# Graph kernel: first edge pass by ranges of 32 nodes, and each group of edges gathered once

## The chip, the cores and the metric

The kernel runs on one core of a Trainium2 chip. Its metric is the device time of one execution in microseconds (us). The engines are PE (TensorE, matrix products; PEld is its weight load), DVE (VectorE), ACT (ScalarE), POOL (GpSimd) and SP (SyncE, which here only issues DMAs). Each engine runs its own list of instructions in order; semaphores tie them together. SBUF is the memory on the chip with 128 partitions, PSUM the eight banks that PE writes.

## What is computed

A graph with 3125 nodes of 128 features and 100,000 edges, sorted by destination in the input, with 64 features an edge. Two message-passing layers, each followed by a residual and a layer norm:

```python
h = x @ node_fc_W + node_fc_b;  he = ea @ edge_fc_W + edge_fc_b
hs, hd = h[src], h[dst]
a = sum(hs * hd, -1)                                    # one score an edge
g = sigmoid(relu(he @ rel_att_W1[m] + b1[m]) @ W2[m] + b2[m])   # m = 0..2
alpha, beta = seg_softmax(a, dst), seg_softmax(g, dst)
h_att = segment_sum(alpha * (hs @ node_att_W[k]), dst) / 3      # over k
h_rel = segment_sum(beta[m] * (hs @ rel_att_W[m]), dst) / 3     # over m
h_red = relu(concat(h_att, h_rel) @ out_fc_W + out_fc_b)
gate = sigmoid(x @ gate_W + gate_b)
x1 = layernorm(x + gate * where(deg > 0, h_red, h) + (1 - gate) * x)
# second layer: edges are summed by src, rows are gathered by dst
e = tanh((x1 @ Wq)[src] + (x1 @ Wk)[dst]);  s = exp(e @ Wphi - max)
out = layernorm(x1 + segment_sum(s / z[src] * ((x1 @ Wy_w + Wy_b)[dst] + e @ We), src))
```

## The kernel before

**Stages, one after the other.** Stage 1 (from L182): SP loads weights, edges and x; 25 blocks of 125 nodes go through `h = x @ W` (PE L470 to L486) and are stored as rows (`h_table`, L372) and transposed (`hT_table`, L373); then the edge MLP runs over 100 octs of 1000 edges (PE L526, L536, L547, ACT L667), which gives three weights an edge. Beside it DVE sorts the edges' keys by source for the second pass (with PE transposes, L564), and counts how many edges belong to nodes below each block's border (L769, 25 passes over the edges), from which a plan of steps is made. The edges' records of 10 words (source, destination, weights as floats and as three bf16 parts) are written to DRAM as `rec0` by five stores (L378), each behind conversions (L853 to L857).

**First edge pass** (L923 to L1155). Edges are in groups of 512 (4 x 128); a step is one group against one block of 125 nodes. Since the edges are sorted, a group crosses few borders: 196 groups and 25 blocks give 196 + 25 - 1 = 220 steps, and a group that crosses a border is loaded and gathered again for the next block. In a step
- SP loads the group's records `rec` and the block's transposed `h`, `hbT` (L972, L973);
- POOL gathers the 512 source rows of `h_table` into `hs` with four indirect DMAs of 128 rows (L984; `hs` has RING = 5 slots in the `arena`), and waits before it until step n - 5 is done (`stepped`);
- DVE makes the one-hot matrix edge to node, `onehot` (L1101, L1104), the one-hot weighed by three relation weights, 128 x 1500 (`weigh`, L1111), the running maximum (`maximum`, L1121 to L1130), and adds the step's sums to the block's (`take`, L1140 to L1145);
- PE transposes the rows (L1000) and the one-hot (L1006), computes scores of 125 nodes x 512 edges (L1017), transposes the exponentials (`turn_back`, L1022), and sums: relations 4 x 375 columns (L1030), their weights' sums (L1033), attention 4 x 129 columns (L1039);
- ACT copies the transposed rows to SBUF (`hsT`, L1061), makes the mask (L1063), copies the transposed exponentials (L1069), and takes the exponentials (L1073, L1075).

The order on PE in one iteration k is `turn_back(k)`, `turn(k+2)`, `scores(k+1)`, `relations(k)`, `attention(k)`. Every step is one iteration of a loop that is written out 10 times.

**Between the passes** (L1160 to L1403): the node update, the layer norm, and the tables of the second layer: `kv_table` with 192 floats a node, and `q_table`.

**Second edge pass** (L1408 to L1676). Again 220 steps, now with the edges sorted by source. SP loads `rec_sb` and `qb` (L1468, L1469); POOL gathers 4 x 128 rows of `kv_table` (L1482) into `row_v` (5 slots), again with waits for the step's records and for step n - 5. PE transposes the one-hot (L1498, copied by ACT L1572), spreads the queries (L1511), DVE adds them to the gathered rows (L1617), ACT takes the tanh (L1552), DVE the scores and the highest of them (L1633 to L1639, L1625) with a transpose and a broadcast on PE (L1518, L1522), ACT the exponentials (L1562 to L1567), DVE spreads them (`spread_p`, L1646), PE sums the messages (L1528), DVE adds them up (`take`, L1658). The tail (L1681 to L1809) normalises and stores the output (L1718).

## Time and profile before

| what | value |
|---|---|
| median of the runs | 3890.93 us (3888.9 to 3900.16, 3 runs) |
| the profiled execution | 3869.89 us, of it 3868.0 us span in the trace |
| mean granted TensorE clock | 0.837 of full speed |

The profile is of one execution. It has a page with busy times per engine, a digit strip over the span, the costliest groups of instructions, and the DMA queues; the trace behind it can be asked for the instructions of a stretch (a timeline), for busy times by stretch (windows), for what each engine waited for (waits). Busy shares of an engine are averages over stages that have different limits. "issue" as releaser means that the engine waited for nothing that the profile shows; "remote" that a semaphore released it whose setter the profile can't name.

### The profile page before, as it was taken

Reading aid. Unit: us, or ns where it says so; the run is one execution under the profiler, and the core shown is the slowest. Engines: PE = TensorE matmul, PEld = TensorE weight load, DVE = VectorE, ACT = ScalarE, POOL = GpSimd, SP = SyncE. Lnnn points to the kernel's source line nnn. Section 1 sums busy time; section 2 is a strip of 40 time slices with the busy share of each in tenths; the row PEclk is TensorE's granted clock in tenths of the full one; section 3 lists DMA queues with packets and bytes.
Section 4 is the critical chain, followed back from the end, with each engine's and each line's share of the span. In section 5 each row is a group of like instructions: output and inputs, shape, how many; then the busy total and the mean of one; then the engine's idle time right before and its main releaser. Section 6 shows DMA issues by size and latency. Waiting matters only on the chain. (4 is left out here: it accounts for less than half of the span.)

```text
span 3868.0 us, 66746 instructions
## 1 busy us (share of the span) xinstructions
PE 2980.1 (77%) x17025; PEld 2039.3 (53%) x17025; DVE 2193.4 (57%) x5947; ACT 1479.6 (38%) x3759; POOL 1902.0 (49%) x1791
## 2 busy tenths in 40 slices
PE   5999999698989889898889936665665666656663
PEld 3444333466666666666666634554554555545552
DVE  8455210566666656666656673655555555555554
ACT  3777776233333334333333322222222222222221
POOL 0000000566666656666656502666666666666660
PEclk9999999799999989999999965776667777677675
DMA  2111121212212112222212102222222222222220
GB/s 69 57 45 45 55 76 39 60 48 52 52 49 50 50 47 52 49 52 51 49 48 50 39 2 60 72 70 70 70 71 72 70 70 71 71 71 72 71 69 19
DMA packets 231858, 217.93 MB, mean 56 GB/s; under 512 B 161623, under 2 KB 190124, under 8 KB 231787
## 3 DMA queue, kind: packets, MB, share of 16 engines
q0 software_dynamic: 70400, 144.29, 14.0%
q1 hardware_dynamic: 161387, 72.74, 7.5%
q8 instruction: 38, 0.62, 0.1%
q14 instruction: 33, 0.27, 0.0%
HBM read 203.65 MB, written 13.22 MB: 56 GB/s over the span
## 5 line engine op out<-in xcount | busy, mean ns | idle before, releaser
L984 POOL DMA_INDIRECT arena<-h_table,rec x880 | 976.4, 1110 | 545.8 <-issue 249.9
L1482 POOL DMA_INDIRECT arena<-kv_table,rec_sb x880 | 911.8, 1036 | 471.7 <-issue 235.3
L1030 PE MATMUL bank<-arena 128*128 128x375 f32 x1760 | 611.3, 490 | 0.0
L1528 PE MATMUL bank<-arena,probT 128*125 128x193 f32 x1760 | 513.8, 456 | 122.3 <-DVE probT L1646 65.6
L1528 PEld LDWEIGHTS bank<-arena,probT 128*125 128x125 f32 x1760 | 422.8, 265 | 179.7 <-DVE probT L1646 103.3
L1030 PEld LDWEIGHTS bank<-arena 128*128 128x128 f32 x1760 | 349.4, 199 | 302.0 <-issue 122.6
L1522 PE MATMUL bank<-top_run,ones 1*128 1x1 f32 x440 | 108.6, 313 | 367.8 <-DVE top_run L1625 196.4
L1111 DVE TENSOR_TENSOR arena<-onehot,rec 128x1500 f32<-128x1500 bf16 x220 | 376.5, 1711 | 0.0
L536 PE MATMUL bank<-eaT,wc 64*128 64x500 f32 x1200 | 360.8, 616 | 0.0
L1572 ACT COPY hotT<-bank 125x512 bf16<-125x512 bf16 x220 | 128.1, 582 | 580.4 <-remote 514.3
L1126 DVE CUSTOM_DVE_ANT_0 score<-bank,mask,m_old 125x512 f32<-125x512 f32 x220 | 165.2, 751 | 296.3 <-remote 178.8
L1522 PEld LDWEIGHTS bank<-top_run,ones 1*128 1x128 f32 x440 | 89.9, 253 | 453.2 <-DVE top_run L1625 243.1
L667 ACT ACTIVATE arena<-bank,bias 128x500 f32<-128x500 f32 x534 | 314.6, 684 | 36.6 <-PE bank L536 32.3
L977 POOL MEMSET arena<- 128x20 f32 x1 | 0.1, 134 | 649.5 <-POOLq L328 649.5
L1069 ACT COPY probT<-bank 128x500 f32<-128x500 f32 x220 | 126.8, 576 | 439.3 <-PE bank L1022 309.4
L1073 ACT ACTIVATE prob<-score,m_neg 125x512 f32<-125x512 f32 x220 | 158.8, 722 | 343.4 <-DVE m_neg L1129 308.6
L1022 PE MATMUL bank<-identf,prob 125*128 125x125 f32 x880 | 146.5, 292 | 165.5 <-issue 95.2
L1017 PE MATMUL bank<-hsT,hbT 128*125 128x512 f32 x440 | 272.0, 704 | 0.0
L1039 PE MATMUL bank<-arena,probT 128*125 128x129 f32 x1760 | 248.6, 283 | 0.0
L1617 DVE TENSOR_TENSOR arena<-bank,arena 128x256 f32<-128x256 f32 x220 | 92.7, 421 | 245.3 <-remote 235.9
L536 PEld LDWEIGHTS bank<-eaT,wc 64*128 64x128 f32 x1200 | 133.1, 186 | 164.1 <-ACT arena L667 105.9
L1646 DVE TENSOR_TENSOR probT<-onehot,p_e 128x500 f32<-128x500 bf16 x220 | 149.7, 680 | 115.9 <-ACT p_e L1565 80.1
(291 smaller groups left out, 4881.7 us busy)
## 6 DMA issues: line engine op xcount, KB each, us to landing
ea<-in_edge_attr SPq DMA_DIRECT2D x100, 250.0 KB
arena<-h_table,rec POOLq DMA_INDIRECT x880
arena<-kv_table,rec_sb POOLq DMA_INDIRECT x880
hbT<-hT_table SPq DMA_DIRECT2D x220, 62.5 KB
qb<-q_table SPq DMA_DIRECT2D x220, 46.9 KB
rec<-rec SPq DMA_DIRECT2D x220, 20.0 KB
rec<-rel_st SPq DMA_DIRECT2D x5, 781.2 KB
rec_sb<-rec SPq DMA_DIRECT2D x220, 4.0 KB
```

The costliest lines, as they stand in the source:

```text
L536: pe.matmul(bank[1 + (6 * o + n) % 4][:, 0:4 * LANES], wc[half * DE:(half + 1) * DE, m * D:(m + 1) * D], eaT[half * DE:(half + 1) * DE, o ...
L667: act.activation(hid[o % 3 * 6 + n], bank[1 + (6 * o + n) % 4][:, 0:4 * LANES], ACT.Relu, bias=bias1[:, m:m + 1]).then_inc(hid_sb, 1)
L984: pool.indirect_dma_start(out=hs[:, k % RING, j, 0:D], out_offset=None, in_=h_table, in_offset=bass.IndirectOffsetOnAxis(ap=rec_v[:, k, j, ...
L1017: pe.matmul(bank[2][0:BN, :], hbT[:, k, :], hsT[:, k % 2, :], start=True, stop=True).then_inc(score_ps, 1)
L1030: pe.matmul(bank[6 + k % 2][:, 0:M * BN], hs[:, k % RING, j, 0:D], hot_w_v[:, k % 2, j, :], start=(j == 0), stop=(j == GT - 1))
L1039: last = pe.matmul(bank[4 + k % 2][0:BN, 0:D + 1], probT_v[:, k % 2, j, :], hs[:, k % RING, j, :], start=(j == 0), stop=(j == GT - 1))
L1073: act.activation(prob[:, k % 2, :], score[:, k % 2, :], ACT.Exp, bias=m_neg[:, k % 2:k % 2 + 1]).then_inc(prob_done, 1)
L1111: v.tensor_tensor(hot_w[:, k % 2, :].rearrange("p (j m n) -> p j m n", j=GT, m=M), onehot_v[:, k % RING, :, :].unsqueeze(2).to_broadcast([ ...
L1126: v.tensor_tensor_reduce(score[:, q, :], bank[2][0:BN, :], mask[:, q, :], 1.0, m_old[:, q:q + 1], ALU.add, ALU.max, m_new[:, q:q + 1]).the ...
L1482: pool.indirect_dma_start(out=row_v[:, k % RING, j, 0:KV], out_offset=None, in_=kv_table, in_offset=bass.IndirectOffsetOnAxis(ap=rec_v[:, ...
L1522: pe.matmul(bank[3][:, 0:1], ones[0:1, :], top[0:1, k:k + 1], start=True, stop=True).then_inc(top_ps, 1)
L1528: last = pe.matmul(bank[4 + k % 2][0:BN, 0:KV + 1], probT_v[:, k % 2, j, :], row_v[:, k % RING, j, AD:RK], start=(j == 0), stop=(j == GT - 1))
```

## The change

**Nodes in blocks of 128.** BN is 128 in place of 125, 25 blocks, the last one part full; tables have 3200 rows. In the x phase each block has 4 ACT copies instead of 6, with PSUM banks for two blocks.

**Edge records stay in SBUF.** Sources, destinations and weights of all edges lie in SBUF by group (`src_g`, `dst_g`, `w_g`); the record stores and conversions are gone. SP loads `dst_g` and `src_g` in runs of 4 words, 128 x 195 runs for each, right behind the first four loads of edge features and ahead of the stores of `h_table` and `hT_table`; ACT waits for all of those stores before the edge MLP. The MLP runs over 98 octs of 1024 edge slots. The counting passes are 98 (one a range border) instead of 25.

```diff
-                        sp.dma_start(ea[:, k, :], ea_dram[:, o * 8 * DE:(o + 1) * 8 * DE]).then_inc(ea_in[k], 16)
+                        def load_group(table, name):
+                            sp.dma_start(table[:, 0:COLS - GT].rearrange("p (g j) -> p g j", j=GT),
+                                         i[name][0:FULL].rearrange("(g p j) -> p g j", p=128, j=GT)).then_inc(groups_in, 16)
...
+                        for o in range(U):
+                            load_edges(o)
+                        load_group(dst_g, "dst")
+                        load_group(src_g, "src")
+                        for b in range(NB):
+                            sp.wait_ge(hT_sb, b + 1)
+                            sp.dma_start(h_table[b * BN:(b + 1) * BN, :], h_sb[:, b, :]).then_inc(h_out, 16)
+                            sp.dma_start(hT_table[:, b * BN:(b + 1) * BN], hT[:, b, :]).then_inc(h_out, 16)
```

**First pass by ranges of 32 nodes.** A step is one group against one of 98 ranges of 32 nodes: 196 + 98 - 1 = 293 steps, rounded up to 296 (`STEPS0`). POOL goes over the 196 groups, written out, and gathers each once into a ring of 16 landed groups (`RING0`, `landed_rows`); before group g it loads from `reach_row` the last step that uses group g - 16 and waits for it. SP copies a step's rows by DMA from the ring into one of 8 step slots (`hs`, 128 x 516 floats) and loads 32 columns of `hT_table`:

```diff
+                        groups = sp.value_load(plan_s[0:1, bass.ds(n, 1), 0], min_val=1, max_val=GROUPS)
...
+                        sp.wait_ge(stepped, n + SU0 - SH + 1)
+                        sp.wait_ge(ready, groups)
...
+                        sp.dma_start(hbT[:, k, :], hT_table[:, bass.ds(within(col, (WINS - 1) * WN), WN)]).then_inc(step_in[k], 16)
+                        sp.dma_start(hs[:, k, :, :].rearrange("p j d -> p (j d)"),
+                                     landed_rows[:, bass.ds(within(at, (RING0 - 1) * GT), GT), :].rearrange("p j d -> p (j d)")).then_inc(step_in[k], 16)
```

On PE the scores' tile is 32 x 512. The mask is made in PSUM by two products ahead of the scores (a constant from `far`, and the one-hot times a large diagonal), so ACT's mask is gone. The probabilities (32 columns a group of 128) and the one-hot weighed by three relation weights (96 columns) stand side by side in `both`, and one product a quarter gives all sums of the step, 128 x 129:

```diff
+                        pe.matmul(tile, far[0:1, 0:WN], far[0:1, WN:], start=True, stop=False)
+                        for j in range(GT):
+                            pe.matmul(tile[:, j * 128:(j + 1) * 128], onehot_v[:, k % SH, j, :], big_ident[:, :], start=False, stop=False)
+                        pe.matmul(tile, hbT[:, k % SH, :], hsT[:, k % 2, :], start=False, stop=True).then_inc(score_ps, 1)
...
+                            last = pe.matmul(bank[4 + k % 4][:, 0:D + 1], both[:, k % 4, j, :], hs[:, k % SH, j, :],
+                                             start=(j == 0), stop=(j == GT - 1))
```

The order on PE in iteration k is `turn_back(k+1)`, `scores(k+3)`, `turn(k+4)`, `sums(k)`. ACT takes the exponentials straight from PSUM. DVE makes a 128 x 128 one-hot and a 128 x 384 weighed one, takes the minimum of the negated scores (one instruction), and has one sum to add instead of three. What stands in a row on PE, before:

```order
L1030 MATMUL bank<-arena 128x375 x4
L1033 MATMUL bank<-rec,onehot 125x9 x4
L1039 MATMUL bank<-arena,probT 125x129 x4
L1022 MATMUL bank<-identf,prob 128x125 x4
L1000 MATMUL bank<-identf,arena 128x128 x4
L1004 REGISTER_ALU
L1006 MATMUL bank<-identb,onehot 125x128 x4
L1017 MATMUL bank<-hsT,hbT 125x512
```

and now (`big_ident` is the diagonal, `hs` the step's rows):

```order
L1026 MATMUL bank<-identf,prob 128x32 x4
L1034 REGISTER_ALU
L1037 MATMUL bank<-far 32x512
L1039 MATMUL bank<-big_ident,onehot 32x128 x4
L1040 MATMUL bank<-hsT,hbT 32x512
L1048 MATMUL bank<-identf,hs 128x128 x4
L1056 MATMUL bank<-hs,both 128x129 x4
```

The relations' 375 columns and their sums have left the iteration, and the constant's product has come in. On POOL in the first pass, before, the gathers of two steps:

```order
L984 DMA arena<-h_table,rec 128x128 x4
L981 REGISTER_ALU
L984 DMA arena<-h_table,rec 128x128 x4
L981 REGISTER_ALU
L984 DMA arena<-h_table,rec 128x128 x4
```

and now the gathers of two groups:

```order
L1007 TENSOR_LOAD reach_row
L1007 ISA x2
L1008 REGISTER_ALU
L997 DMA area_b<-h_table,src_g 128x128 x4
L1007 TENSOR_LOAD reach_row
L1007 ISA x2
L1008 REGISTER_ALU
L997 DMA area_b<-h_table,src_g 128x128 x4
```

Each set of four gathers has a value load ahead of it; a step no longer has a set of its own.

**Second pass.** The 220 steps stay. POOL gathers each of the 196 groups once into a ring of 8 (`RING1`), with the sources of indices loaded once (`rec_all`), and SP moves a step's rows by DMA (128 x 4 x 192 floats) into the `row_v` slots; DVE's `add_queries` waits for that DMA (`moved`).

```diff
-                            pool.wait_ge(loaded[k], 32 * s + LOADS0 + 32)
-                            pool.wait_ge(stepped, s * SU + k + SU - RING + 1)
...
+                        sp.wait_ge(stepped, n + SU - RING + 1)
+                        sp.wait_ge(ready, groups)
...
+                        sp.dma_start(row_v[:, k % RING, :, 0:KV], landed_rows[:, bass.ds(at, GT), :]).then_inc(moved[k % RING], 16)
...
-                        v.wait_ge(gathered[k % RING], 64 * turn_of(s, k) + GATHERS0)
+                        v.wait_ge(moved[k % RING], 16 * turn_of(s, k))
```

On SP, one step before (the loads of records and queries with the values they need):

```order
L1465 TENSOR_LOAD plan_row1
L1465 ISA x2
L1466 ISA
L1466 TENSOR_LOAD plan_row1
L1466 ISA x2
L1467 REGISTER_ALU
L1468 ISA
L1468 DMA rec_sb<-rec 128x8
L1469 ISA
L1469 DMA qb<-q_table 125x192
```

and now the part that stands behind the same loads of the step five ahead:

```order
L1433 DMA qb<-q_table 128x192
L1437 ISA
L1437 TENSOR_LOAD plan_l
L1437 ISA x2
L1438 ISA
L1438 TENSOR_LOAD plan_l
L1438 ISA x2
L1442 ISA
L1442 DMA sum_acc<-sum_acc 128x4x192
```

The move of the rows (named `sum_acc` after the area that holds both rings) is a third DMA on SP's queue in each step, with two more value loads.

**Between and after.** The node update transposes four sums a block (the relations are in rows of the same area), accumulates four products in PSUM and adds the bias once, in place of a chain of four additions a block. The output is stored as 24 blocks of 128 nodes and one of 53.

## Rows read from the trace of the kernel before

**Rows 1.** Page, busy time, share of the span, instructions.
```profile
PE 2980.1 (77%) x17025; PEld 2039.3 (53%) x17025; DVE 2193.4 (57%) x5947; ACT 1479.6 (38%) x3759; POOL 1902.0 (49%) x1791
```

**Rows 2.** Windows: stretch, length, busy of PE, PEld, DVE, ACT, POOL, PEclk, DMA share, GB/s.
```profile
100.00:655.00 555.00, 550.20 (x2880) 221.56 (x2880) 183.60 (x329) 406.35 (x727) 0.00 (x0) 1.00 0.17 54
697.00:2224.00 1527.00, 1358.02 (x7476) 974.11 (x7476) 975.80 (x2419) 578.47 (x1100) 970.21 (x874) 0.93 0.20 50
2390.00:3787.00 1397.00, 879.68 (x5939) 721.08 (x5940) 804.47 (x2638) 396.89 (x1540) 911.68 (x880) 0.71 0.27 70
```

**Rows 3.** Timeline of PE in the first pass: start, duration, engine, line, what, [idle before].
```profile
1604.53 1.09 PE L1022 MATMUL bank<-identf,prob 125*128 125x125 f32 x4 [4.12 <-issue]
...
1611.65 0.59 PE L1022 MATMUL bank<-identf,prob 125*128 125x125 f32 x4
1612.07 0.60 PE L1000 MATMUL bank<-identf,arena 128*128 128x128 f32 x4
1612.51 0.39 PE L1006 MATMUL bank<-identb,onehot 128*125 128x128 bf16 x4
1612.74 1.07 PE L1017 MATMUL bank<-hsT,hbT 128*125 128x512 f32 x2
1613.65 2.69 PE L1030 MATMUL bank<-arena 128*128 128x375 f32 x8
1616.18 0.34 PE L1033 MATMUL bank<-rec,onehot 128*125 128x9 bf16 x4
1616.38 1.13 PE L1039 MATMUL bank<-arena,probT 128*125 128x129 f32 x8
1617.35 0.59 PE L1022 MATMUL bank<-identf,prob 125*128 125x125 f32 x4
```

**Rows 4.** Waits: engine, what, its line, releaser: us in total, times, longest.
```profile
ACT hotT L1572 <- remote: 514.3, 107, 8.4
...
POOL arena L1482 <- remote: 182.8, 86, 3.7
...
PE bank L1022 <- issue: 95.2, 33, 4.4
```

**Rows 5.** Page, groups of gathers: busy us, mean ns of one, idle before.
```profile
L984 POOL DMA_INDIRECT arena<-h_table,rec x880 | 976.4, 1110 | 545.8 <-issue 249.9
L1482 POOL DMA_INDIRECT arena<-kv_table,rec_sb x880 | 911.8, 1036 | 471.7 <-issue 235.3
```

**Rows 6.** Timeline of POOL in the first pass.
```profile
1408.64 1.65 POOL L984 DMA_INDIRECT arena<-h_table,rec  x1 [0.30 <-issue]
```

**Rows 7.** Timeline of all engines in the second pass.
```profile
2997.73 0.42 PE L1498 MATMUL bank<-identb,onehot 128*125 128x128 bf16 x4
...
3002.23 0.95 POOL L1482 DMA_INDIRECT arena<-kv_table,rec_sb  x1 [0.30 <-issue]
...
3006.01 0.59 ACT L1572 COPY hotT<-bank 125x512 bf16<-125x512 bf16 x1 [5.86 <-remote]
...
3006.92 1.27 POOL L1482 DMA_INDIRECT arena<-kv_table,rec_sb  x1 [2.49 <-remote]
```

**Rows 8.** Timeline of PE at the end of the second pass, behind POOL's last gather.
```profile
3779.39 1.57 PE L1528 MATMUL bank<-arena,probT 128*125 128x193 f32 x8 [0.65 <-DVE probT L1646]
...
3782.70 1.57 PE L1528 MATMUL bank<-arena,probT 128*125 128x193 f32 x8 [0.23 <-DVE probT L1646]
```

**Rows 9.** Page, the group of the weighed one-hot on DVE.
```profile
L1111 DVE TENSOR_TENSOR arena<-onehot,rec 128x1500 f32<-128x1500 bf16 x220 | 376.5, 1711 | 0.0
```

**Rows 10.** Timeline of SP: a load that blocks its queue, and the output store.
```profile
13.15 15.59 SPq L353 DMA_DIRECT2D w<-in_L_gnn_rel_att_W  x1
...
3851.40 0.31 SPq L1718 DMA_DIRECT2D out<-y_sb  x1
```

**Rows 11.** Page, DMA queue of SP: packets, MB, share of 16 engines.
```profile
q1 hardware_dynamic: 161387, 72.74, 7.5%
```

**Rows 12.** Timeline of DVE at the end of stage 1.
```profile
683.85 0.06 DVE L1091 MEMSET neg_big<- 125x1 f32 x1 [8.53 <-PEq L328]
```

1316 lines of the change are left out of this document (651 added, 665 removed).

## Prediction

> **What bounds the kernel now.** I read the page's busy shares first: TensorE is busy 77% of the span [rows 1]. An average over unlike stages says little, so the second look was at the busy times by stage [rows 2]. In the edge MLP (100 to 655 us) PE is busy 550 of 555 us: PE binds. In the first edge pass (697 to 2224) PE is busy 1358 of 1527 us at a mean granted clock of 0.93, POOL 970; in the second pass (2390 to 3787) PE has 880 of 1397 us at 0.71 and POOL 912: neither is full. So each pass needs the timeline of its steps.
>
> A first-pass step that waits for nothing shows each matmul group by its start [rows 3]: 0.42 for the probability transposes (L1022), 0.44 for the row transposes (L1000), 0.23 and 0.91 for one-hot transposes and scores, 2.53 for the three relations (L1030), 0.20 for their sums and 0.97 for the attention, together 5.70 us. 220 such steps would make 1254 us; the stage took 1527, that is 6.9 a step. The missing 1.2 us a step are slower steps and pauses like that ahead of 1604.53, where PE sat for 4.12 us and the profile names no releaser [rows 3]; there are 33 of this kind at that line, 95 us in all [rows 4].
>
> What are they? POOL issues a gather of 128 rows in 1.110 us on average in the first pass and 1.036 in the second [rows 5], and 0.30 us lies between two [rows 6]: at least 4 x 1.34 = 5.4 us of a step is POOL's own. The second pass shows best how the others fare in that time [rows 7]: the one-hot transposes at 2997.73 take 0.42 us, yet ACT, free for 5.86 us, copies their result only at 3006.01, 7.9 us after they ended. POOL issued its gathers back to back the whole time and resumes at 3006.92, after 2.49 us of rest. The waits repeat it: the copy L1572 waits 107 times for a "remote" release, 514 us in total, and POOL waits 86 times, 183 us [rows 4]. Once POOL has issued its last gather, the same steps follow each other in 3.3 us (from 3779.39 to 3782.70) [rows 8]. I read this as a release by PE that arrives late while POOL issues without a rest. The second pass is then bound by POOL's 5.3 us plus a share of late releases (6.3 us a step), the first by PE's 5.7 us plus some.
>
> **First pass, the change.** Steps go from 220 to 296 (196 groups and 98 ranges of 32 nodes, less one, rounded up to a multiple of 8); 3 of them are empty. PE per step, by the rows of [rows 3]: four probability transposes have 32 output columns instead of 125 (at least a quarter of 0.42, at most all: I take 0.25); the K=1 matmul that adds the far constant has 512 columns in bf16 (the 0.23 of four 128-column bf16 groups: 0.21), the one-hot product is of the same size as the one-hot transposes (0.22); scores 0.91, since the 512 columns stay; row transposes 0.44; the sums are 4 x 129 columns as the attention is, 0.97, and now hold relations and attention stacked in the 128 rows: the 2.53 + 0.20 go. Sum 3.0 us, x 296 = 888 us against 1254, at full clock. Behind a pause, at the lower of the two clocks, L1022 takes 1.09 us in place of 0.59 [rows 3]; at a mean clock of 0.71, as in the second pass now, PE would need about 4.1 us a step.
>
> POOL: 196 groups in place of 220 steps, so 784 gathers: 784 x (1.110 + 0.30) = 1105 us. Each group adds a value load and its waits; the trace has none on POOL, and I take 0.5 us, between one gap of 0.30 us and two (bounds 0.3 and 0.7): 1203 us (1164 to 1242). DVE had 976 us for 220 steps [rows 2], 4.4 each, of which 1.71 is the weighing of 1500 elements a lane [rows 9]; it now has 384, and there is one sum instead of three: under 3 us, not a bound. The rows' copy from the landing ring (264 KB a step, 78 MB in all) is on SP's queue; the DMA engines are busy 0.20 of the stage [rows 2] and the copy would at most double or treble that. SP issues two DMAs and three loads a step, some 2 us by 0.31 us for an issue [rows 10] and as much for a load with its register work: hidden, and a bound only above 4 us.
>
> Ends of the range per step: POOL alone 1203/296 = 4.06; the late releases on top. In a step the path PE turn, ACT copy, PE scores, DVE minimum, ACT exp, PE transposes, ACT copy, PE sums is spread over four iterations, so each release may be late by about one iteration less the work without a stall. POOL now waits for nothing before 16 groups, so it has fewer rests than today, which speaks against the change. I take 4.3 us a step, near POOL's floor, because PE's pauses are few today (33 at L1022 in 220 steps) in spite of POOL: 1273 us. From 1527 that is **-254** (bounds -345 by POOL without slowing by DVE, to +515, the rival D).
>
> One rule bears on POOL's term. The row at 1408.64 shows a gather of 1.65 us between gathers of 0.95 us [rows 6]. The Trainium skill ("SBUF — State Buffer", section "SBUF: two separate sides") says that VectorE operations in a two-port mode keep GpSimd from writing the descriptors of its DMAs. No row here shows which operation did it, but the 1.71-us weighing would be the candidate, and it becomes a quarter as long: by the rule POOL's gathers shrink to 784 x 1.25 = 980 us, by the row's mean they stay at 1105. The sum uses 1105.
>
> **Second pass.** PE, ACT and DVE do the same per step; POOL's 880 gathers become 784, 784 x (1.036 + 0.30) = 1047 us, + 196 x 0.5 = 1145. The gathers no longer wait for a step's records nor for the step five before it, but for the group eight before it; between gather and use stands a DMA of 393 KB a step (86 MB), issued by SP behind the loads of the step five ahead. With 3.3-us steps possible without POOL [rows 8], POOL's stream is the floor: 1145/220 = 5.2 us. Late releases hold up the steps, and now POOL does not rest with them until the ring of eight is full, so part of the 183 us of rests [rows 4] goes and part comes back as waits of PE. I take 5.6 us a step with the ramp, 1252 in place of 1397: **-145** (bounds -226 at POOL's floor, 0 if the loop's late releases set the pace as now).
>
> **Ahead of the first pass.** Group loads of dst and src now stand on SP's queue ahead of the 50 stores of h, and ACT waits for all those before the edge phase. They are 2 x 24,960 runs of 16 bytes. SP's queue moved 161,387 packets in 7.5% of 16 engines' span [rows 11]: 28.8 ns a packet, which gives 49,920 x 28.8 / 16 = 90 us; packets that small should cost less than the mean, so 45 to 90, and I take 67. They are issued at about 32 us (the queue is blocked to 28.7 by one load [rows 10]) and land at 99; 50 stores at 0.31 to 0.5 us behind them end near 124. The edge phase starts at 100 today: +25 (-15, if the shorter x phase sets it, to +50). The Trainium skill ("DMA: Bandwidth & Descriptors", sections "Specifications" and "Measured") wants runs of 512 bytes for line rate and gives a floor of about 10.5 ns a packet; 33 us by that as an estimate, and the edge phase would begin 10 us early. No row shows 16-byte runs. The MLP has 98 x 1024 edge slots for 100 x 1000: +2. The last conversions and store of the records (DVE idles 8.53 us for it [rows 12]) go: -10. Counting is now 98 passes over the edges instead of 25; DVE is idle for 371 of the 555 us of the MLP [rows 2] and hides them. Sum **+17** (-25 to +45).
>
> **Between the passes and after.** The 166 us between the windows [rows 2] lose the relation matmuls of the node update and gain transposes: **-15** (-30 to +5). The output store, from 3851.40 to the end at 3868 [rows 10], has 128 partitions for 125, and its 16.6 us should come nearer to half: **-8** (0 to -10).
>
> **Sum.** 17 - 254 - 15 - 145 - 8 = -405 against the span 3868: 3463. The profiled execution (3869.89) is 21 us below the median of the runs: forecast **3480**. Measurements of this kernel can tell 0.3% (12 us) from no change.
>
> **Rivals.**
> B, POOL's stream is all there is: both passes at its floor with fewer slow gathers, first pass 1182 and second 1171. 3868 + 17 - 345 - 15 - 226 - 8 = 3291, about **3300** with the offset. For it: the pauses of PE are few in today's first pass [rows 4]; against: the late releases [rows 7].
> C, the second pass gains nothing: its steps wait for PE's releases, and those come when POOL rests, however few groups it gathers. 3868 + 17 - 254 - 15 - 8 = 3608, **3630**.
> D, the slower side: a late release costs its time per step, not per group. If a first-pass step stays at 6.9 us as today, because POOL issues on and the scores wait for ACT's copy that waits for PE's release, 296 of them are 2042 us, +515; 3868 + 17 + 515 - 15 - 145 - 8 = 4232, **4250**. It decides from where the pass grows over 1527 + 151 us, that is from 5.7 us a step. For it: [rows 7], 7.9 us for one release; against: PE's own 5.70-us rhythm [rows 3] breaks seldom today with two iterations of lead [rows 4], and the new order has four.
> E, gains and costs about cancel (steps of 5.6 to 5.7 us).
>
> **Chances.** Forecast 0.44 (its own range 3380 to 3570), B 0.19, C 0.22, D 0.11, E 0.04 (0.03 of it within 0.3%, the rest faster). Faster by over 0.3% 0.86, within 0.03, slower 0.11. The range 3280 to 3700 leaves out D, E and a little of B.
>
> **What would show it.** The first pass over 296 steps at 4.1 to 4.6 us with POOL busy nearly without gaps, PE groups without L1030's 2.5 us, PE clock under 0.9: right. Steps above 5 us with ACT's copy of the turned rows (the old L1061) waiting for "remote": D's mechanism. A second pass of 1397 us or more: C. The first edge matmul later than 150 us or earlier than 85: the group loads are mis-sized. The row copies binding would show as a DMA share over 0.8, and SP's issue rows without a pause. Most wrong would be the take of 4.3 us, which rests on how long a release is late, and no row prices that for four iterations of lead.

## The result, and the profile after

The changed kernel takes 4143.58 us (median of 4 runs, 4118.61 to 4162.02) where the kernel before takes 3889.91 us (median of 4): a ratio of 1.0644, with a 95% interval of 1.0569 to 1.0719. It is slower by 6%; 3480 us had been forecast, and the time lies outside the range of 3280 to 3700.

In the experiments the same two kernels also ran on other chips, and there the change is a gain. **c_after** took 3112.51 us (median) beside 3387.46 us for the kernel before (ratio 0.919, interval 0.9174 to 0.9205). The experiments ran on four chips: on two of them the kernel before took 3388 to 3396 us, on the other two, and on the chip of the result, 3843 to 3890. I call the second kind "chips with late releases", for the reason that follows; the prediction rests on a trace of that kind, and so does the result above. Of the experiments, those without an interval were run once.

So there are four traces to read: before and after on a chip of each kind. One group of matmuls a step marks the passes: the attention sums (L1039), now the joint sums (L1056), and the messages (L1528, now L1525). Each row gives the shortest, median and longest duration in ns, then the start of the first and the last. The kernel before, late releases:
```profile
L1039 PE MATMUL bank<-arena,probT x1760: 271/273/354, 712.8 to 2223.3; 128*125 128x129 f32 x196
L1528 PE MATMUL bank<-arena,probT x1760: 324/528/688, 2413.2 to 3787.1; 128*125 128x193 f32 x196
```
The changed kernel, late releases:
```profile
L1056 PE MATMUL bank<-hs,both x2368: 272/275/423, 766.5 to 2428.0; 128*128 128x129 f32 x198
L1525 PE MATMUL bank<-sum_acc,probT x1760: 324/528/691, 2638.1 to 4086.9; 128*128 128x193 f32 x196
```
The changed kernel on a chip without late releases (c_after):
```profile
L1056 PE MATMUL bank<-hs,both x2368: 272/275/422, 706.0 to 1692.1; 128*128 128x129 f32 x198
L1525 PE MATMUL bank<-sum_acc,probT x1760: 324/528/691, 1870.3 to 3037.5; 128*128 128x193 f32 x196
```
The kernel before on the same chip (c_before):
```profile
L1039 PE MATMUL bank<-arena,probT x1760: 271/273/354, 713.0 to 1960.7; 128*125 128x129 f32 x196
L1528 PE MATMUL bank<-arena,probT x1760: 324/528/687, 2143.3 to 3303.8; 128*125 128x193 f32 x196
```
By their medians the single matmuls are equally long on both kinds, only the spans differ. In us, a pass from the first to the last start, divided by 219 steps (220 less one) or, in the new first pass, by 295:

| | late: before | late: after | without: before | without: after |
|---|---|---|---|---|
| first sums at | 713 | 767 | 713 | 706 |
| first pass | 1510 (6.90 a step) | 1662 (5.63) | 1248 (5.70) | 986 (3.34) |
| from there to the first messages | 190 | 210 | 183 | 178 |
| second pass | 1374 (6.27) | 1449 (6.62) | 1161 (5.30) | 1167 (5.33) |
| from there to the end | 81 | 73 | 81 | 73 |
| span | 3868 | 4160 | 3385 | 3111 |

The columns add up: with late releases the change costs 54 + 151 + 20 + 75 - 8 = +292 us, without them it gives -7 - 262 - 4 + 7 - 8 = -274.

Busy times by stage, the changed kernel with late releases, then without (columns as in [rows 2]):
```profile
698.00:2428.00 1730.00, 1240.53 (x6801) 752.35 (x6799) 538.16 (x1475) 519.02 (x1479) 760.23 (x763) 0.76 0.24 77
2584.00:4087.00 1503.00, 969.88 (x5940) 784.91 (x5940) 810.05 (x2638) 404.30 (x1541) 782.98 (x784) 0.65 0.40 117
```
```profile
698.00:1692.00 994.00, 988.61 (x6792) 625.66 (x6793) 539.65 (x1472) 494.44 (x1479) 736.12 (x764) 1.00 0.44 133
1846.00:3037.00 1191.00, 857.24 (x5936) 683.04 (x5937) 802.84 (x2639) 417.04 (x1541) 803.01 (x786) 0.75 0.52 147
```
Without late releases PE is busy 988.61 of 994 us in the first pass, at full clock. With them it has 1240.53 of 1730 us at 0.76: the same matmuls, with pauses and, behind the pauses, a lower clock. The waits of the changed kernel with late releases (columns as in [rows 4]):
```profile
ACT hotT L1569 <- remote: 555.4, 141, 6.6
...
DVE junk L1133 <- remote: 527.2, 82, 29.3
...
ACT hsT L1079 <- remote: 485.5, 78, 29.4
...
DVE sum_acc L1614 <- DMA sum_acc<-sum_acc: 450.5, 188, 35.4
```
In the first pass DVE waits 527.2 us for scores and ACT 485.5 us for turned rows, and in the second ACT waits another 555.4 us, each time for a release that the profile can put down to no setter. In c_after and c_before no wait has "remote" as its releaser at all.

The start of the first pass shows most plainly what a late release is. POOL has 16 free slots there and issues 64 gathers one behind the other, every 1.25 us, from 671.7 to 752. The changed kernel with late releases, SP and DVE in that time (timeline of SP, then of all engines):
```profile
708.21 0.69 SPq L983 DMA_DIRECT2D hbT<-hT_table  x1
...
726.57 0.70 SPq L983 DMA_DIRECT2D hbT<-hT_table  x1
...
731.67 0.74 DVE L1133 TENSOR_SCALAR_CACHE_REDUCE junk<-bank,m_old 32x512 bf16<-32x512 f32 x1 [29.26 <-remote]
...
742.85 0.59 ACT L1079 COPY hsT<-bank 128x512 f32<-128x512 f32 x1 [29.44 <-remote]
...
768.49 1.25 POOL L997 DMA_INDIRECT area_b<-h_table,src_g  x1 [16.50 <-PE bank L1056]
```
SP, which waits for nothing here, needs 18.36 us from one step's `hbT` load to the next (708.21 to 726.57); DVE waits 29.26 us for scores whose matmul started at 713.48, and ACT, free since 713.42, copies only at 742.85 what PE turned from 729.41 to 730.50. At 768.49 POOL has waited 16.50 us for a step. The same place without late releases:
```profile
697.10 0.35 SPq L983 DMA_DIRECT2D hbT<-hT_table  x1
...
700.08 0.35 SPq L983 DMA_DIRECT2D hbT<-hT_table  x1
```
2.98 us from load to load, with POOL gathering all the same. The record of the trace also holds SP's register instructions, which the timeline leaves out: between the two loads at 708.21 and 726.57 nearly all of them last 0.69 to 0.73 us each, where the same ones, but for the value loads, last 0.02 to 0.16 us between 697.10 and 700.08 in c_after. What of a chip makes the difference I don't know. The gathers themselves are alike, 995 ns on average with late releases (page, busy us and mean ns) and 964 in c_after:
```profile
L997 POOL DMA_INDIRECT area_b<-h_table,src_g x784 | 780.3, 995 | 1538.1 <-issue 871.3
```

### The profile page after: what moved, and what is told of

It is laid out like the page before. It is cut to its first block and busy times, and to the rows that moved or that the text cites. A ratio compares the mean times of both kernels' runs of the same rounds, so it can differ in the third digit from the quotient of the medians.

```text
span 4160.4 us, 66648 instructions
## 1 busy us (share of the span) xinstructions
PE 2957.8 (71%) x16380; PEld 1891.6 (45%) x16380; DVE 1804.8 (43%) x5054; ACT 1411.6 (34%) x4020; POOL 1575.7 (38%) x1602
## 5 line engine op out<-in xcount | busy, mean ns | idle before, releaser
L997 POOL DMA_INDIRECT area_b<-h_table,src_g x784 | 780.3, 995 | 1538.1 <-issue 871.3
L1465 POOL DMA_INDIRECT sum_acc<-kv_table,rec_all x784 | 783.6, 1000 | 686.1 <-PE bank L1525 405.4
L1525 PE MATMUL bank<-sum_acc,probT 128*128 128x193 f32 x1760 | 597.0, 514 | 30.6 <-DVE probT L1643 19.4
L1133 DVE TENSOR_SCALAR_CACHE_REDUCE junk<-bank,m_old 32x512 bf16<-32x512 f32 x296 | 218.4, 738 | 815.6 <-remote 527.2
L1525 PEld LDWEIGHTS bank<-sum_acc,probT 128*128 128x128 f32 x1760 | 498.8, 309 | 95.2 <-DVE probT L1643 73.1
L1040 PE MATMUL bank<-hsT,hbT 128*32 128x512 f32 x592 | 399.6, 765 | 0.0
L1056 PE MATMUL bank<-hs,both 128*128 128x129 f32 x2368 | 365.8, 304 | 0.0
L678 ACT ACTIVATE sum_acc<-bank,bias 128x512 f32<-128x512 f32 x588 | 351.3, 696 | 40.3 <-PE bank L557 35.9
L557 PE MATMUL bank<-area_b,wc 64*128 64x512 f32 x1176 | 362.8, 635 | 0.2 <-ACT sum_acc L678 0.2
L1056 PEld LDWEIGHTS bank<-hs,both 128*128 128x128 f32 x2368 | 346.9, 224 | 0.9 <-issue 0.8
L1569 ACT COPY hotT<-bank 128x512 bf16<-128x512 bf16 x220 | 128.9, 586 | 608.9 <-remote 555.4
L1048 PE MATMUL bank<-identf,hs 128*128 128x128 f32 x1184 | 244.7, 342 | 53.0 <-DMA hs<-area_b 26.6
```

The lines of the kernel that those rows point to most:

```text
L557: pe.matmul(bank[1 + (6 * o + n) % 4][:, :], wc[half * DE:(half + 1) * DE, m * D:(m + 1) * D], eaT[half * DE:(half + 1) * DE, o % 3, :], s ...
L678: act.activation(hid[o % 3 * 6 + n], bank[1 + (6 * o + n) % 4][:, :], ACT.Relu, bias=bias1[:, m:m + 1]).then_inc(hid_sb, 1)
L997: pool.indirect_dma_start(out=landed_rows[:, k * GT + j, 0:D], out_offset=None, in_=h_table, in_offset=bass.IndirectOffsetOnAxis(ap=src_g[ ...
L1040: pe.matmul(tile, hbT[:, k % SH, :], hsT[:, k % 2, :], start=False, stop=True).then_inc(score_ps, 1)
L1048: last = pe.transpose(bank[0][:, j * 128:(j + 1) * 128], hs[:, k % SH, j, 0:D], identf[:, :])
L1056: last = pe.matmul(bank[4 + k % 4][:, 0:D + 1], both[:, k % 4, j, :], hs[:, k % SH, j, :], start=(j == 0), stop=(j == GT - 1))
```

## The experiments

Theory A: while POOL issues gathers one behind the other, releases and instructions of the other engines are held up on some chips. Theory B: a step's own chain is the bound. For the second pass, theory S: SP's list of instructions fills the step; theory M: the latency of the row move. The two passes are separated by a barrier, so one kernel can carry an edit in each. Runs with the same time of the kernel before beside them ran on one chip; each section names its kind by that time. e1, e2, f1 and g3 leave out work (most gathers), so their sums are of old rows: only their times are read.

**e1, no gathers** (3388 us beside it, no late releases). Edit, in the first pass, and with `RING1` in the second:

```diff
+                        if g >= RING0:
+                            return
```

> The changed kernel, but POOL issues gathers only for the first 16 groups of the first pass and the first 8 of the second; later groups keep their waits and their release, so the rows used are stale (work left out: 720 and 752 gathers). Theory A (POOL's back-to-back gathers hold up the releases and the instructions of every other engine, SP's above all): behind the first 16 groups a first-pass step takes 3.1 us, as now in intervals without a gather, so from the first scores to the last sums some 70 + 290 x 3.1 = 970 us instead of 1730; a second-pass step takes 3.3 to 4 us, 730 to 880 us instead of 1449; total near 2750. Theory B (the step's own chain, its row copy by DMA and SP's instructions, is the bound, and the gathers only run beside it): the first pass stays above 1500 us, the second above 1300, total above 3900.

3094 us. First and second pass:
```profile
L1059 PE MATMUL bank<-hs,both x2368: 272/275/377, 705.8 to 1685.7; 128*128 128x129 f32 x198
L1531 PE MATMUL bank<-sum_acc,probT x1760: 324/528/690, 1865.7 to 3019.4; 128*128 128x193 f32 x196
```
3.32 and 5.27 us a step, but c_after has 3.34 and 5.33 with all gathers. On this chip they cost nothing, so A wasn't tested; what the run shows is B for this kind of chip, and that the second pass has a bound of 5.3 us that is not POOL. Here it shows on SP's queue, with one row move in each step:
```profile
2501.61 0.67 SPq L1445 DMA_DIRECT2D sum_acc<-sum_acc  x1
...
2506.84 0.67 SPq L1445 DMA_DIRECT2D sum_acc<-sum_acc  x1
```
5.23 us from row move to row move, the pace of the pass.

**e2, memsets for gathers** (same chip). As e1, with nine (seven) memsets of the slot in place of a group's gathers.

> As e1, but in place of the left-out gathers POOL fills the group's slot with memsets, nine a group in the first pass and seven in the second, about the 5 us that four gathers take. Theory A with the descriptor writing of the gathers as cause: steps as short as in e1 unless POOL's own pace (about 5 us a group, 980 us a pass) binds, so 1000 to 1100 us a pass. Theory A with POOL's mere being busy, or its turning of the ring, as cause: near the changed kernel, 1730 and 1449 us.

3367 us; 3.96 and 5.65 us a step. POOL's memsets, chained by waits, take 6.0 us a group where four gathers take 5.07, and set the first pass. Nothing was held up on this chip, so this run says nothing of A either.

**e3, a rest behind each gather** (same chip).

```diff
+                            rested_n[0] += 1
+                            pool.memset(rest, 0.0).then_inc(rested, 1)
+                            pool.wait_ge(rested, rested_n[0])
```

> The changed kernel with a rest of POOL behind each gather: a memset of 256 words and a wait for it, some 0.35 us, so that two gathers never follow at once. Theory A: releases of the others get through in the rests; the gathers take 784 x 1.6 us = 1250 plus 100 for value loads, and the first pass becomes 1350 to 1450 us instead of 1730 although POOL does more; second pass 1350 to 1450 instead of 1449. Theory B, or a POOL that holds others up in proportion to its gathers: no shorter than now, or longer by up to 270 us a pass.

3913 us, 4.98 and 6.75 us a step: slower, since nothing was held up here and POOL binds. Four gathers take 7.5 us instead of 5.07 (784 of them from 670.5 to 2148.5); I read this as its sequencer no longer running ahead.

**e4, offset gathers, and the old gather in the second pass** (same chip).

```diff
+                            if j == 2 and last_step is not None:
+                                pool.wait_ge(stepped, last_step + SU0 + 2)
...
-                        if inside(edge, k, 0):
-                            move_rows(s, k)
...
+                            pool.wait_ge(stepped, s * SU + k + SU - RING + 1)
+                            for j in range(GT):
+                                pool.indirect_dma_start(
+                                    out=row_v[:, k % RING, j, 0:KV], out_offset=None, in_=kv_table,
```

> Two edits in stages that are separated by a barrier. First pass: the last two gathers of a group wait one step longer than the first two, so that runs of gathers are shorter. Theory A: 1350 to 1650 us instead of 1730; theory B: 1730. Second pass: the old way, four gathers a step straight into the step's slot (880 instead of 784), and no row moves on SP's queue. If the second pass lost by the row move and what SP does for it, it is back at 1371 us from its first to its last messages (1449 now); if blocks of 128 nodes or anything else costs it, it stays near 1449.

3105 us. The second pass took 1163 us with the old gathers and 1167 with ring and row moves: where POOL's gathers had taken 5.3 us (four of 1.018 us and 0.30 us behind each, c_before), SP's list now takes as long. What surprised more was the first pass, 3.34 us, far below what I had read in the trace, and the 3388 us of the kernel before. That led to the next two.

**c_after, c_before** (3387 us, no late releases). No edit.

> The changed kernel unchanged, as the measure for the four runs before it, beside which the kernel before took 3388 us where it had taken 3890. In the experiment with offset gathers no engine waited for a late release and SP's instructions took 0.04 us beside gathers, where the changed kernel's trace has 0.70. If that comes from the edit (shorter runs of gathers), this run has steps of 5.6 us in the first pass and 6.6 in the second, and takes some 4140 us, 1.2 times the kernel before beside it or more. If it comes from where or when it ran, the late releases are gone here too: 3.34 us a step in the first pass, 5.3 in the second, near 3110 us, 0.92 of the kernel before.

> The kernel before, for its trace beside that of c_after. If it takes 3388 us again and the 500 us are the late releases, then the first pass has 5.7 us a step nearly throughout (1254 us in all, not 1510) and the second about 5.3 (1165, not 1371), and waits for remote releases are near nil. If the 500 us are something else (clock, a faster stage 1), those passes are as long as in the first trace.

3112.51 and 3387.17 us: the late releases were gone in both kernels, and the edits of e4 had no part in it.

**e5 and e6, SP's list shorter and longer** (3889 us beside them: late releases).

```diff
-                            g = sp.value_load(plan1_row[0:1, bass.ds(n * 2, 1)], min_val=0, max_val=GROUPS - 1)
-                            b = sp.value_load(plan1_row[0:1, bass.ds(n * 2 + 1, 1)], min_val=0, max_val=NB - 1)
+                            g, b = values(mybir.EngineType.SP, plan1_row[0:1, bass.ds(n * 2, 2)], GROUPS - 1)
```

> The changed kernel; in the second pass SP reads group and block of the next step with one load of two values instead of two loads. In the trace of c_after SP never waits in the second pass: its list of some 30 instructions fills 5.3 us a step, and without any gather (e1) a step takes 5.26 too. Theory S (SP's list is the bound there): 0.9 us less of it gives 4.4 us, and then POOL's gathers bind at 784 x 1.27 / 220 = 4.5 us: second pass 1000 to 1050 us instead of 1167, total near 2960 to 3000 where the changed kernel takes 3112. Theory M (the latency of the row move, or the chain through the step five back, is the bound): 1167 us as now.

```diff
+                        for _ in range(2):
+                            sp.value_load(plan_s[0:1, bass.ds(n, 1), 0], min_val=1, max_val=GROUPS)
...
+                        sp.value_load(plan_l[0:1, bass.ds(n, 1), 0], min_val=1, max_val=GROUPS)
```

> The changed kernel with loads on SP whose values nobody uses: two more a step in the first pass (about 0.6 us each), one more in the second. Theory S: second pass 5.3 + 0.6 = 5.9 us a step, +130 us; first pass, where SP's list fills 2.95 of 3.34 us, goes to 4.1 to 4.2 us a step, +230 us; total near 3470, slower than the kernel before. Theory M, SP hidden: no change, 3112.

The expectations were for the other kind of chip, so the passes have to be set beside the changed kernel with late releases. e5 took 4047.97 us (ratio to before 1.0421, interval 1.0366 to 1.0476), e6 4310.71. Their messages, e5 and then e6:
```profile
L1535 PE MATMUL bank<-sum_acc,probT x1760: 324/528/691, 2601.8 to 3975.0; 128*128 128x193 f32 x196
```
```profile
L1528 PE MATMUL bank<-sum_acc,probT x1760: 324/528/690, 2672.0 to 4235.5; 128*128 128x193 f32 x196
```
Second pass 1373 and 1564 us against 1449: one load less gives 76 us, one more costs 115. That is S, on this kind of chip too. How far such passes scatter from run to run shows in the first pass, which e5 leaves as it is (1645 us, the changed kernel 1662), and in f4 below, which has e5's second pass (1351 us, e5 1373): some 20 us. In the first pass e6 took 1692 us: two loads more cost 30 to 47 us, so there SP's list is not the bound on this kind of chip. For comparison with f4, e5's first pass:
```profile
L1056 PE MATMUL bank<-hs,both x2368: 272/275/423, 765.1 to 2410.5; 128*128 128x129 f32 x198
```

**f1, no gathers, merged load** (3850 us beside it: late releases). e1's and e5's edits.

> As e1 (gathers only for the first 16 groups of the first pass and the first 8 of the second, the rest left out) with SP's merged load of e5. Chips differ: some show late releases beside gathers (the kernel before takes 3890 us there), some do not (3388 us). Where they do, theory A (the gathers' issue holds up the others' releases and instructions) says: without gathers both passes run as on the other chips, 3.32 us a step in the first, 4.4 in the second, total near 2900 us, against 4048 for the same kernel with gathers. If such a chip is slow for another reason, the passes stay above 5 us a step. On a chip without late releases: first pass 3.32 us as in e1, second 4.4 us (5.26 in e1) if SP's list is its bound, total near 2910.

2923.3 us; the kernel with gathers (e5) takes 4048.
```profile
L1059 PE MATMUL bank<-hs,both x2368: 272/275/398, 764.0 to 1744.0; 128*128 128x129 f32 x198
L1541 PE MATMUL bank<-sum_acc,probT x1760: 324/327/691, 1932.1 to 2848.4; 128*128 128x193 f32 x196
```
3.32 and 4.18 us a step: on a chip with late releases, without gathers, the first pass runs as on the other kind. Theory A holds there, B falls. In the second pass the gathers cost 457 us (1373 in e5, 916 here), far more than the 76 us of a load. The first sums still come at 764.0, since the 16 first groups were gathered in one run: 58 us later than the 705.8 of e1. The second pass at 4.18 us instead of e1's 5.27 is S again, with less on SP's list.

**f3, a short rest** (same chip). A memset of one word a partition behind each gather, without a wait.

> The changed kernel with the merged load, and behind each gather a memset of one word a partition on POOL, so that gathers follow each other at about 1.4 us instead of 1.25. Where releases are late, theory A: a short rest lets them through; the first pass is bound by POOL at 784 x 1.4 = 1100 us, 3.7 to 4.2 us a step instead of 5.6, the second 5.0 to 5.8 instead of 6.3; total 3450 to 3700 instead of 4048. Rival A2 (releases are late in proportion to the gathers, rests change nothing): 4048 or more. On a chip without late releases: slower than without the rest, 3.75 us a step in the first pass (+120 us).

4048.67 us (ratio 1.0514, interval 1.0482 to 1.0545), the time of e5 (first pass 1684 us, second 1346). The memset was no rest:
```profile
1500.36 0.95 POOL L998 DMA_INDIRECT area_b<-h_table,src_g  x1 [0.19 <-issue]
1501.31 0.11 POOL L1002 MEMSET area_b<- 128x1 f32 x1
1501.61 0.94 POOL L998 DMA_INDIRECT area_b<-h_table,src_g  x1 [0.19 <-issue]
```
It fits into the 0.30 us that lie between gathers anyway, which still start every 1.25 us. The run says nothing of rests.

**f4, offset gathers, merged load** (same chip). e4's first edit and e5's.

> The changed kernel with the merged load, and in the first pass the last two gathers of a group wait one step longer than the first two. Where releases are late, theory A: shorter runs of gathers, first pass 4.2 to 5.2 us a step instead of 5.6; total 3750 to 3950 instead of 4048. Rival A2: 4048. On a chip without late releases: first pass 3.34 us as before (e4), second pass 4.5 to 4.7 us instead of 5.3 by theory S, total near 2960 to 2990 and the fastest of all so far; by theory M 3112.

3819.6 us (ratio 0.9901, interval 0.9865 to 0.9936): first pass 1459 us, 4.94 us a step, where e5 has 1645.
```profile
L1060 PE MATMUL bank<-hs,both x2368: 272/275/423, 763.7 to 2222.3; 128*128 128x129 f32 x198
```
Behind the first sums POOL's gathers come in 191 runs of 3.8 on average (counted from the timeline, a run ending at a pause of 0.5 us or more), in e5 in 108 runs of 6.7. The same gathers in shorter runs cost 186 us less.

**g1 and g3, e3 and e2 again** (3843 us beside them: late releases).

> The same kernel as e3 (a memset of 256 words and a wait for it behind each gather, no other edit), in the hope of a chip with late releases; on the chip without, its steps took 4.97 us in the first pass and 6.74 in the second, bound by POOL. The short rest of f3 was none: the one-word memset fitted into the 0.30 us that lie between gathers anyway, which went on every 1.25 us. Where releases are late: if a real rest of some 0.6 us lets them through (A), the passes are as on the other chip, 4.97 and 6.7 us a step (the first 0.6 less than the changed kernel's 5.6). If the releases are held by the gathers in proportion (A2), it is slower than the changed kernel in both passes, above 6 us a step in the first.

3915.61 us, where e3 took 3913 on the other kind, and the passes are alike too, 1471 and 1477 us against 1468 and 1477. With a real rest behind each gather the difference between the chips is gone. Even the first sums come at 711.1 behind the same 64 gathers (710.8 in e3). POOL in g1, with a gather every 1.55 us in a group and a longer pause between groups:
```profile
1501.24 0.95 POOL L999 DMA_INDIRECT area_b<-h_table,src_g  x1 [0.27 <-POOL area_b L1003]
1502.19 0.33 POOL L1003 MEMSET area_b<- 128x256 f32 x1
1502.79 0.95 POOL L999 DMA_INDIRECT area_b<-h_table,src_g  x1 [0.27 <-POOL area_b L1003]
...
1507.14 0.95 POOL L999 DMA_INDIRECT area_b<-h_table,src_g  x1 [1.53 <-issue]
```

> The same kernel as e2 (POOL busy with memsets about as long as the gathers, which are left out behind the first groups). On the chip without late releases: 3.96 us a step in the first pass, 5.64 in the second, first sums at 708 us. Where releases are late: if it is the gathers' own work that holds releases up, the same 4.0 and 5.6 us; if any busy POOL does, 5.6 and 6.6 us as in the changed kernel.

3403.61 us against 3367 for e2; 3.83 and 5.59 us a step, with waits for a remote release only at the real gathers that open the passes. A busy POOL holds nobody up; gathers in a row do. Whether it is their issue or their transfers that does it, no run separates. The 64 gathers at the start are real in this kernel, and its first sums come at 767.0 (708.4 in e2).

**g2, gathers spread over the steps, and h2, the same again.** g2 ran beside g1 (3843 us, late releases), h2 beside 3396 us (no late releases). With the merged load of e5:

```diff
                         for j in range(GT):
+                            ahead = 4 * g + j - 40
+                            if ahead > 0:
+                                pool.wait_ge(stepped, SU0 + ahead * STEPS0 // (GT * GROUPS) + 1)
+                                pool.sem_inc(ticks, 1)
```

> The changed kernel with the merged load, and POOL's gathers spread over the steps: gather q of a pass waits until (q - 40) x 296/784 steps are done in the first pass, (q - 24) x 220/784 in the second, so at most three gathers follow each other in the first pass, and the burst of 64 at its start is gone. Where releases are late: A says 3.7 to 4.3 us a step in the first pass (5.6 in the changed kernel), 5.3 to 5.9 in the second, the start of the pass 40 us shorter; total 3450 to 3650, under the kernel before by 5 to 10%. A2 says no gain over f4 (3820). On a chip without late releases: 3.34 to 3.5 and 4.6 to 4.8 us a step, total 2970 to 3030.

> g2 again. On a chip with late releases 3680 to 3710 us, 0.96 of the kernel before, as measured. On a chip without (kernel before 3388 us): first pass 3.34 to 3.5 us a step, second 4.6 to 4.8, total 2970 to 3030, 0.88 to 0.89 of the kernel before, which would make it the fastest on both kinds of chip; if the waits for steps hold POOL up there, 3112 (the changed kernel) or more.

g2: 3695.96 us, ratio 0.9607 (0.9548 to 0.9666). h2: 2993.28 us, ratio 0.8813 (0.8797 to 0.8828).
```profile
L1060 PE MATMUL bank<-hs,both x2368: 272/275/423, 737.3 to 2143.0; 128*128 128x129 f32 x198
L1543 PE MATMUL bank<-sum_acc,probT x1760: 324/528/690, 2331.3 to 3626.4; 128*128 128x193 f32 x196
```
```profile
L1060 PE MATMUL bank<-hs,both x2368: 272/275/377, 708.3 to 1691.2; 128*128 128x129 f32 x198
L1543 PE MATMUL bank<-sum_acc,probT x1760: 324/328/690, 1866.1 to 2916.2; 128*128 128x193 f32 x196
```
With late releases the first pass takes 1406 us (1645 in e5) and the second 1295 (1373). Without them 983 and 1050: the waits for steps cost nothing, and 5.33 us a step in the second pass became 4.79, inside what S had given (4.6 to 4.8); since the gathers cost nothing on this chip, I put it down to SP's shorter list, though no run here had the shorter list without the spreading. On both kinds of chip this is the fastest version of those that do all the work. With late releases it took 46 us more than the top of the forecast: the runs of gathers are 3.4 long on average in the first pass, but runs of five to seven still occur (POOL, g2):
```profile
1499.35 1.24 POOL L1001 DMA_INDIRECT area_b<-h_table,src_g  x1 [1.89 <-PE bank L1060]
...
1504.64 0.94 POOL L1001 DMA_INDIRECT area_b<-h_table,src_g  x1 [0.30 <-issue]
1507.70 0.94 POOL L1001 DMA_INDIRECT area_b<-h_table,src_g  x1 [2.12 <-remote]
```

**h1, spread gathers with a rest** (beside h2, no late releases).

> g2 with a real rest behind each gather, a memset of one word and a wait for it: by g1's rows (0.95 gather, 0.33 memset, 0.27 idle) some 1.33 us from gather to gather instead of 1.25, and about 1.2 us more at each group's end, since POOL's sequencer can no longer run ahead: 6.5 us a group. Where releases are late: in g2 some remain (80 waits of DVE for a remote release, 331 us). A says the rests let them through, and POOL's pace binds: 6.5 x 196/296 = 4.3 us a step in the first pass (4.76 in g2), 5.8 in the second (5.91), total near 3540 to 3600 where g2 takes 3696. If the rest is too short to help: 3700 or more. On a chip without late releases: slower than g2, 4.3 and 5.8 us a step, near 3300.

4246.95 us (ratio 1.2507, interval 1.2484 to 1.253), far from the 3300 expected: the gathers now start every 1.9 us:
```profile
1504.87 0.94 POOL L1003 DMA_INDIRECT area_b<-h_table,src_g  x1 [0.83 <-POOL area_b L1007]
...
1506.76 0.94 POOL L1003 DMA_INDIRECT area_b<-h_table,src_g  x1 [0.83 <-PE bank L1065]
```
I had taken the pause behind the memset from g1's rows, 0.27 us; with two waits between two gathers it is 0.83. Whether a cheaper rest would take away what is left in g2 stays open.

## Why the prediction was wrong

**The reading of the bound was right, and its price was wrong.** I had read in the trace of before that PE's releases come late while POOL issues without a rest [rows 7]; f1, g1 and g3 show for the changed kernel that releases are late behind gathers in a row. Then I took 4.3 us a step for the first pass, 0.24 us over POOL's floor of 4.06, "because PE's pauses are few today". That is the step that failed: a step takes 5.63 us, and of these 2.29 are the price of late releases, with the lower clock behind their pauses (0.76 against 1.00), since it takes 3.34 where none is late. The pauses that I had counted were those of one engine at one line (33 at L1022, 95 us); in the same trace DVE alone waited longer for late scores:
```profile
DVE score L1126 <- remote: 178.8, 46, 9.2
```
The price was in my own text. PE's 5.70 us were 1.2 short of the measured step, and c_before, with 5.70 us a step, shows that these 1.2 us were what late releases cost the old kernel. On top of the floor they would have given 4.06 + 1.2 = 5.3 us a step and 1557 us, no gain in this pass. I had also called PE the old pass's bound alone; POOL's four gathers are as long (4 x 1.41 = 5.6 us), and in c_before POOL never pauses for 0.5 us between the first sums and the last.

**Why a step pays 2.29 us now and paid 1.2 before stays open.** I had written that POOL "has fewer rests than today, which speaks against the change". In number it does: behind the first sums its first-pass gathers come in 108 runs, 6.7 long on average and at most 8 but for the 64 that open the pass, where the kernel before has 155 runs of 5.6, the longest 20. f4 and g2 show that more and shorter runs help. But in sum POOL rests longer than before, 669 us against 316, because it waits for the steps. Before and now, both with late releases:
```profile
POOL arena L984 <- PE bank L1039: 195.6, 87, 5.2
```
```profile
POOL area_b L997 <- PE bank L1056: 642.2, 92, 16.5
```
And in the second pass the runs became shorter (from 6.7 to 4.2 on average) while the step became longer. So the length of the runs is not the whole of it. The new step also hangs on a row copy by SP, whose own instructions are held up, has another order on PE and little more than half of PE's work; no run separates these, gives the ring the old depth, or takes the gathers out of the kernel before.

**Rival D came nearest, with a chance of 0.11.** Its sign appeared: ACT's copy of the turned rows waits for "remote", 78 times. Its price did not: 78 such waits in 296 steps are not one a step, and a step does not stay at 6.9 us. From the first to the last sums it is 5.63 us; by the window that D was reckoned in (1527 us, now 1730, which takes in the later start) it is 5.8, just past D's point of decision at 5.7. The forecast gain of the second pass, which D kept, did not come either: it took 75 us more. That 4144 us lie near D's 4250 is therefore in part luck. Of the 1049 us between the spans of the two columns "after" of the table, the kernel before has 483: what late releases cost in all has more than doubled.

**First pass, term by term.** Where releases are not late, -262 us were measured and -254 forecast, which is luck: the forecast goes from 6.9 us a step to 4.3, that chip from 5.70 to 3.34. PE's step was forecast at 3.0 us and is 3.34. POOL's floor was too high: a group takes 5.07 us (784 gathers from 672.2 to 1665.7 in c_after), so the 0.5 us for a value load and waits was nothing, and I read this as POOL's sequencer doing them while a gather is being issued. (The bound of -345 in the prediction can't be got from its terms: gathers of 980 us and 98 for the groups make 1078, which is -449.) And gathers became shorter, 1121 ns in c_before and 964 in c_after (1110 and 995 with late releases). The change also shortened VectorE's weighing of the one-hot, from 1711 to 552 ns. The Trainium skill ("SBUF — State Buffer", "SBUF: two separate sides") says that GpSimd is kept from writing its DMA descriptors while VectorE runs an operation that takes the shared port pair. That would fit; no run shortened the weighing alone, so it is not shown.

**Second pass: -145 forecast, +75 with late releases, +7 without.** I costed POOL and left SP at nothing, a second term that failed. The row move put a third DMA and two value loads on its list, which fills 5.3 us a step, as much as POOL's gathers had. Where no release is late, e1 shows this bound (5.27 us with no gathers); f1, again without gathers but with one load less, has 4.18 us, and h2 agrees. Where releases are late, e5 and e6 move the pass with the list, but the gathers weigh more (457 us between e5 and f1). SP's instructions themselves are held up there: of its some 3940 register instructions in this pass 7.6% last 0.5 us or more, in c_after none, and they add up to 410 us against 245. The step grew to 6.62 us. My rival C (no gain, because the steps wait for late releases) gave the right size where none is late, for another reason; where they are late its reason is not excluded.

**Ahead of the passes.** +25 us had been forecast for the start of the edge phase; it starts at 79.45 us, 20 us earlier than before, under the 85 us that I had named as the sign of mis-sized group loads. 7 of the 20 are left at the first sums where releases are not late. SP's queue shows the two group loads blocking it, 32 us from 24.54 to 56.47 (rows from the second issue on):
```profile
25.05 16.06 SPq L386 DMA_DIRECT2D dst_g<-in_dst  x1
...
41.58 14.84 SPq L386 DMA_DIRECT2D src_g<-in_src  x1
56.47 0.36 SPq L395 DMA_DIRECT2D h_table<-h_sb  x1
```
I had taken 67 us from the mean packet of [rows 11]. The Trainium skill ("DMA: Bandwidth & Descriptors", "Measured"), with its 10.5 ns a packet, had given an estimate of 33 us, and the trace agrees with that: a mean over packets of mixed sizes was the wrong row for the smallest. The 50 stores behind them end at 80: 24 us for them, as costed.

**Between and after.** -4 us were measured without late releases (-15 forecast), +20 with them. The update between the passes did shorten as forecast, by 11 to 12 us up to POOL's first gather (154 to 155 us from the last sums, 167 before). But the second pass starts with a run of 32 gathers, and from the first of them to the first messages it now takes 55 us with late releases (23 before) and 24 without (16 before). The output store gave the 8 us forecast.

## What to carry to other kernels

Price a stall by what the whole step has lost to it, and not by the pauses of one engine at one line: here the missing 1.2 us a step were in the first reading of the trace, and the forecast let them go without a reason that a row bore out. When work moves to the engine that "only issues DMAs", count its list of instructions per step like any other engine's. And let a producer that has slack run evenly rather than as far ahead as its ring allows: the same 784 gathers, spread, took a kernel that was slower than before by 4% (e5) to one that is faster by 4% (g2, on another chip of the same kind), and cost nothing where no release was late (h2).

## What the runs showed of the hardware

Chips differ in how far indirect gathers on POOL's queue hold up the others: with 64 in a row, SP took 18.36 us between the loads of two steps on one chip and 2.98 on another, and the kernel before, unchanged, took 3890 and 3388 us. The kernel with e3's rests took 3913 and 3916 us on the two kinds. Memsets on POOL in place of the gathers held up nobody. Beside late releases SP's register instructions are stretched too: their mean in the first pass is 95 ns in the changed kernel, 54 in c_after, and 54 in f1, which has no gathers there on a chip with late releases; those of the other engines keep their means. A rest of 0.3 us between gathers, which is there anyway, is no help; one of about 0.6 us within a group and more between groups is. What lies between, and what of the chip is at work, was not measured.
